# First tile of a CIN tower: part of slot a's third layer set ahead of slot b's first layer

## The chip, the cores and the metric

The kernel runs on one core of one Trainium2 chip. The metric is the device time of one execution, in microseconds. Of the kernel before there are three runs, 619.76, 620.20 and 620.31 us; the median is 620.2 us.

## The reference, cut to what matters

1024 samples each gather 32 embedding rows of 16 numbers. Three layers of a compressed interaction network follow, each a product with the samples' own embeddings and a contraction, and then a small three-layer network.

```python
x0 = embeddings                       # b samples, m = 32 fields, d = 16
xk = x0
for W in (W0, W1, W2):                # W: 32 x (32 or 64) x 64
    xk = relu(einsum('bmd,bhd,mhk->bkd', x0, xk, W))
    outs.append(sum(xk, axis=2))
z = concatenate(outs, axis=1)
h = relu(concatenate([z, dense_ctx], axis=1) @ W_top1 + b_top1)
h = relu(h @ W_top2 + b_top2)
y = h @ W_top3
```

All numbers are 32-bit floats.

## The kernel before, in words

**Streams and tiles.** The samples are cut into 16 streams of 64. Two streams make a tile: the even one uses slot a of every buffer, the odd one slot b. A stream's data is 1024 columns wide (64 samples by 16). Gathers (POOL, L323) fetch its embeddings, SP stores them in a DRAM scratch (L260), loads them back once as `base` (L278), and 16 more times shifted by different numbers of fields as the 16 chunks of `rolled` (L287).

**One layer.** A layer is a sum over chunks of (chunk of `rolled`) times (layer's input), multiplied by weights. DVE (VectorE) computes products of two chunks in one instruction (L406, into one of three `zd` buffers), reading the layer's input from PSUM (`xk_ps`). POOL (GpSimd) computes products of one chunk (L335, into one of four `zg` buffers), reading it from SBUF (`xk_sb`). PE (TensorE) accumulates them (L570), four matmuls for each chunk. The first layer has four chunks and the squares (L434, L579), the second and third have sixteen. ACT (ScalarE) then evacuates the sum (`evacuate`, L455 to L481): four copies into `xk_ps` and four into `xk_sb` (L472) as input of the next layer, and one into `relu_ab` (L481), which DVE later reduces (L382). For most layers `xk_sb` comes first, for the first layers of slot a `xk_ps`. A third layer is not evacuated this way, but summed by ACT (L451).

**The order.** It is written out by hand. `ORDER` lists phases (stream, layer, part); `CHUNKS` and `CHUNKS_AT` give for each part of a layer how many chunks DVE and how many POOL computes. Every engine runs the phases in the order of the list. In the first tile the phases are (0,0,0), (0,1,0), (1,0,0), (0,2,0), (1,1,0), (0,2,1). In the later tiles the order is another, and it repeats. In this document D0, D1, ... are DVE's product instructions in their order and G0, G1, ... POOL's: D4 to D10 and G0, G1 are (0,1,0); D11, D12 are (1,0,0); D13 to D15 and G2 are (0,2,0); D16 to D22 and G3, G4 are (1,1,0); D23 to D26 and G5 are (0,2,1); D27 begins (1,2,0).

**Gathers.** POOL issues all 256 gathers (16 for each stream) from its own queue, between its products. `GATHERS_AFTER_AT` and `GATHERS_AFTER` say how many follow each product: 4 after G0, 7 after G1, 3 after G2, 3 and 4 after G3 and G4, 7 after G5.

**Waits around the change.** DVE waits for `xk_ps` of the layer before (L397), or for the copy of `base` into `xk_ps` where the layer is the first (L394, made by ACT in `base_to_ps`), for the chunks of `rolled`, and for a free `zd` buffer (L401), that is for PE to have used the product three before. POOL waits for `xk_sb` (L355). A second and a third layer of a slot share one PSUM bank of `acc`, so PE begins the third only after the second was copied to `relu_ab`; this is a wait ahead of part 0 of layer 2. ACT's own order in the first tile is: squares of stream 0, evacuate (0,0), copy of base of stream 1, its squares, evacuate (0,1), (1,0), (1,1).

Of the kernel before, what the change touches and what calls it, by code (L numbers as in the profile page):

```python
# [24 lines left out]
STREAMS = BATCH // SAMPLES  # L25
# [20 lines left out]
CHUNKS = {(0, 0): [(4, 0)], (0, 1): [(4, 0), (10, 2)], (0, 2): [(12, 4)],  # L46
          (1, 0): [(4, 0)], (1, 1): [(14, 2)], (1, 2): [(4, 1), (8, 3)]}

CHUNKS_AT = {(0, 1): [(14, 2)], (0, 2): [(6, 1), (8, 1)], (STREAMS - 1, 2): [(12, 4)]}

ORDER = [(0, 0, 0), (0, 1, 0), (1, 0, 0), (0, 2, 0), (1, 1, 0), (0, 2, 1)]
for _t in range(1, TILES):
    ORDER += [(2 * _t - 1, 2, 0), (2 * _t, 0, 0), (2 * _t - 1, 2, 1), (2 * _t, 1, 0), (2 * _t + 1, 0, 0),
              (2 * _t, 1, 1), (2 * _t + 1, 1, 0), (2 * _t, 2, 0)]
ORDER += [(STREAMS - 1, 2, 0)]

# [3 lines left out]
GATHERS_FIRST = 24  # L60
GATHERS_EARLY = 8
GATHERS_AFTER = {(0, 1, 1): [3, 3], (1, 1, 0): [3, 3], (0, 2, 0): [3, 3, 2, 2], (1, 2, 0): [3], (1, 2, 1): [2, 2, 3]}
GATHERS_AFTER_AT = {(0, 1, 0): [4, 7], (0, 2, 0): [3], (1, 1, 0): [3, 4], (0, 2, 1): [7],
                    (STREAMS - 1, 2, 0): [0, 0, 0, 0]}

GATHERS_MORE = {(2 * t, 1, 1): 3 for t in range(1, 6)}
# [2 lines left out]
def chunks(stream, layer):  # L69
    return CHUNKS_AT.get((stream, layer), CHUNKS[stream % 2, layer])  # L70


class Plan:


    def __init__(self):
        self.dve, self.pool, self.merged = [], [], []
        nd = ng = 0
        for stream, layer, part in ORDER:
            parts = chunks(stream, layer)  # L80
# [23 lines left out]
def last_part(q):  # L104
    stream, layer, part = ORDER[q]
    return part == len(chunks(stream, layer)) - 1


def end_of(stream, layer):

    return ORDER.index((stream, layer, len(chunks(stream, layer)) - 1))


def by_act(stream, layer):

    return layer == 2 and stream < STREAMS - 1


def sums_to(stream, layer):

    return sum(last_part(q) and not by_act(*ORDER[q][:2]) for q in range(end_of(stream, layer) + 1))

# [24 lines left out]
def build_cin_tower(nc, ids, dense_t, tables, w0a, w0b, w12, wtop1, btop1, wtop2, btop2, wtop3, eye, out):  # L147
    with ExitStack() as ctx:
# [94 lines left out]
        def bank_of(stream, layer):  # L243
            return 2 if layer == 0 else stream % 2
# [69 lines left out]
        def _(pool):  # L314
# [12 lines left out]
            def product(q, n, j):  # L327
                stream, layer, _ = ORDER[q]
                s = stream % 2
                if n >= ZG_BUFS:  # L330

                    pool.wait_ge(zg_used, n - ZG_BUFS + 1)
                if layer == 1:
                    pool.wait_ge(rolled_in[s][j], 16 * (stream // 2 + 1))
                nc.gpsimd.tensor_tensor(zg[:, n % ZG_BUFS, :], rolled[:, s, j, :], xk_sb[:, s, :],  # L335
                                        ALU.mult).then_inc(zg_ready, 1)
# [5 lines left out]
            def gathers(n):  # L342
                nonlocal done
                for g in range(done, min(total, done + n)):
                    gather(g)
                    done = g + 1
# [5 lines left out]
            for q, (stream, layer, part) in enumerate(ORDER):  # L352
                if PLAN.pool[q]:

                    pool.wait_ge(xk_sb_ready, 4 * evacuations(*phase_before(stream, layer)))  # L355
                for x, (_, n, j, _) in enumerate(PLAN.pool[q]):
                    product(q, n, j)
                    gathers(GATHERS_AFTER_AT.get(ORDER[q], GATHERS_AFTER.get((stream % 2, layer, part)))[x])
                gathers(GATHERS_MORE.get(ORDER[q], 0))
# [62 lines left out]
        def _(act):  # L422
            def base_to_ps(i):
                s = i % 2
                if i > 1:

                    act.wait_ge(zd_ready, PLAN.dve[end_of(i - 2, 2)][-1][1] + 1)
                act.wait_ge(base_in, 16 * (i + 1))
                for h in range(2):
                    nc.scalar.copy(xk_ps[:, s, h * HALF:(h + 1) * HALF],  # L430
                                   base[:, h * HALF:(h + 1) * HALF]).then_inc(base_ps, 1)

            def squares(i):
                nc.scalar.activation(xk_sb[:, i % 2, :], base[:, :], ACT.Square).then_inc(squares_ready, 1)  # L434

            def wait_end(stream, layer):

                who, n, _, _ = PLAN.merged[end_of(stream, layer)][-1]
                act.wait_ge(zd_used if who == "dve" else zg_used, n + 1)
# [15 lines left out]
            def evacuate(stream, layer):  # L455
                s, bank = stream % 2, bank_of(stream, layer)
                wait_end(stream, layer)
                if layer < 2:
                    copies = [(xk_ps, xk_ps_ready), (xk_sb, xk_sb_ready)]
                    if (s, layer) != (0, 0):  # L460

                        copies.reverse()
                    for dst, ready in copies:
                        for h in range(2):
                            if (stream, layer, h) == (0, 0, 1):
                                if dst is xk_ps:

                                    continue

                                act.wait_ge(xk_ps_ready, 4)  # L470
                            for copy in range(2):
                                nc.scalar.activation(  # L472
                                    dst[copy * MAPS:(copy + 1) * MAPS, s, h * HALF:(h + 1) * HALF],
                                    acc[h * MAPS:(h + 1) * MAPS, bank, :], ACT.Relu).then_inc(ready, 1)
                if layer > 0:

                    act.wait_ge(reduced, sums_to(stream, layer - 1))
                elif stream > 1:

                    act.wait_ge(summed, stream - 1)  # L480
                nc.scalar.activation(relu_ab[:, s, :], acc[:, bank, :], ACT.Relu).then_inc(relu_ready, 1)  # L481
# [22 lines left out]
            act.wait_ge(base_in, 16)  # L504
            squares(0)
            evacuate(0, 0)
            base_to_ps(1)
            squares(1)
            evacuate(0, 1)
            evacuate(1, 0)  # L510
            evacuate(1, 1)
            act.wait_ge(const_in, const_count)
            for t in range(1, TILES):
                a, b, m = 2 * t, 2 * t + 1, t - 1
# [22 lines left out]
            m = TILES - 1  # L537
# [14 lines left out]
        def _(pe):  # L552
# [37 lines left out]
            def zsum(m):  # L590

                pe.wait_ge(reduced, sums_to(2 * m + 1, 1))
                pe.wait_ge(summed, 2 * (m + 1))
                if m > 0:
                    pe.wait_ge(y_ready, m)
                half_sums(m, mlp[0:MAPS, 0:TB], 0)
                half_sums(m, mlp[MAPS:P, 0:TB], 1)
                half_sums(m, mlp[0:MAPS, TB:2 * TB], 2).then_inc(zsum_done, 1)

            def mlp1(m):  # L600
                pe.wait_ge(zsum_sb, 2 * (m + 1))
                for c in range(H1 // P):
                    dst = mlp[:, c * TB:(c + 1) * TB]
                    nc.tensor.matmul(dst, wt1a[:, c * P:(c + 1) * P], z01[:, :], start=True, stop=False)  # L604
                    end = nc.tensor.matmul(dst, wt1b[:, c * P:(c + 1) * P], z2d[:, m * TB:(m + 1) * TB],  # L605
                                           start=False, stop=True)
                end.then_inc(h1_done, 1)

            def mlp2(m):
                pe.wait_ge(h1_sb, 4 * (m + 1))  # L610
                for c in range(H2 // P):
                    for k in range(H1 // P):
                        end = nc.tensor.matmul(mlp[:, c * TB:(c + 1) * TB], wt2[:, k, c * P:(c + 1) * P],  # L613
                                               h1[:, k, :], start=(k == 0), stop=(k == H1 // P - 1))
                end.then_inc(h2_done, 1)

            def mlp3(m):
                pe.wait_ge(h2_sb, 2 * (m + 1))
                for k in range(H2 // P):
                    end = nc.tensor.matmul(mlp[0:1, 0:TB], wt3[:, k:k + 1], h2[:, k, :],  # L620
                                           start=(k == 0), stop=(k == H2 // P - 1))
                end.then_inc(y_done, 1)
# [6 lines left out]
                half_sums(TILES - 1, stage[0:MAPS, 0:TB], 0)  # L629
                half_sums(TILES - 1, stage[MAPS:P, 0:TB], 1).then_inc(last_z01_done, 1)  # L630

            for q in range(6):
                phase(q)
            for m in range(TILES - 1):
                q = 6 + 8 * m
                for x in range(5):
                    phase(q + x)
                phase(q + 5, {2: lambda: zsum(m), 5: lambda: mlp1(m)})
                phase(q + 6, {2: lambda: mlp2(m), 6: lambda: mlp3(m)})
                phase(q + 7)  # L640
            phase(len(ORDER) - 1, {6: last_sums})

            m = TILES - 1
# [70 lines left out]
```

## Time and profile before

| | |
|---|---|
| median of three runs | 620.2 us |
| the profiled execution, device time | 619.78 us |
| its span, first to last instruction | 618.0 us |
| mean granted TensorE clock | 0.994 of full speed |
| PE busy | 562.0 us |
| DVE busy | 554.5 us |
| POOL busy | 468.6 us |
| ACT busy | 299.5 us |

Times in the profile are counted from the start of the span. POOL is the engine that both computes and issues gathers; the 0.30 us between two gathers are not counted as busy. D4 starts at 42.23 us; the first tile's products end on DVE at about 101.4 us, where D27 follows.

### The profile page before, as it was taken

To read this page: it belongs to the slowest core of one execution; us is meant where nothing else is said; L and a number is where in the kernel's file an instruction comes from. 1 tells how busy PE (TensorE), PEld (TensorE's weight loads), DVE (VectorE), ACT (ScalarE), POOL (GpSimd) and SP (SyncE) were. 2 spreads that over 40 slices of the span, in tenths; PEclk is the share of its full clock that TensorE was granted. 3 is DMA by queue.
4 is the path that set the end of the run, shared out by engine and by line. 5 is a ranking of instruction groups with operands and counts; after the bars stand their busy time and mean duration, and the time that the engine had idled before them with its cause. 6 is when DMAs were issued, how large, how long until landed. Compare 5 with 4: busy or idle time off the path is not lost.

```text
span 618.0 us, 8180 instructions
## 1 busy us (share of the span) xinstructions
PE 562.0 (91%) x2752; PEld 206.1 (33%) x2752; DVE 554.5 (90%) x281; ACT 299.5 (48%) x1366; POOL 468.6 (76%) x354
## 2 busy tenths in 40 slices
PE   0058889999999999999999999899998999999997
PEld 0012222334333443334333433234332433334334
DVE  0067899999999999999999999989998999999991
ACT  0021607574357535674366535674346544774331
POOL 6748888888888888888888888888888885125450
PEclk9998999999999999999999999999999999999999
DMA  6297979792699819893699719793498809892000
GB/s 171 79 382 254 394 250 396 241 397 82 209 359 330 294 51 374 297 399 108 218 351 339 299 40 379 265 400 130 171 397 309 329 3 319 316 406 100 1 2 0
DMA packets 54252, 152.02 MB, mean 246 GB/s; under 512 B 9697, under 2 KB 18913, under 8 KB 54210
## 3 DMA queue, kind: packets, MB, share of 16 engines
q1 hardware_dynamic: 46018, 149.39, 64.7%
q0 software_dynamic: 8192, 2.11, 2.6%
q8 instruction: 21, 0.34, 0.2%
q14 instruction: 21, 0.17, 0.1%
HBM read 147.26 MB, written 4.20 MB: 245 GB/s over the span
## 4 chain that ended last, share of the span: by engine, by line
PE 48%; POOL 23%; DVE 10%; issue 9%; DMA 6%; SPq 1%; ACT 1%; DVEq 0%; POOLq 0%
PE acc L570 43%; POOL emb L323 14%; DVE zd L406 10%; POOL zg L335 9%; DMA rolled<-x_scratch 5%; PE mlp L613 2%; SPq L287 1%; PE mlp L604 1%; PE mlp L605 1%; PE acc L579 1%; PE mlp L620 0%; DVE zpart L382 0%; PE mlp L586 0%; ACT xk_sb L472 0%; DMA emb<-tables_in,index 0%
## 5 line engine op out<-in xcount | busy, mean ns | idle before, releaser
L406 DVE TENSOR_TENSOR zd<-rolled,xk_ps 128x2048 f32<-128x2048 f32 x239 | 530.0, 2279 | 16.2 <-PE acc L570 9.2
L570 PE MATMUL acc<-zd,w_sb 128*64 128x512 f32 x1672 | 384.6, 597 | 8.4 <-DVE zd L406 8.4
L323 POOL DMA_INDIRECT emb<-tables_in,index x256 | 244.6, 955 | 75.3 <-issue 64.3
L335 POOL TENSOR_TENSOR zg<-rolled,xk_sb 128x1024 f32<-128x1024 f32 x94 | 223.8, 2382 | 52.0 <-ACT xk_sb L472 18.9
L570 PEld LDWEIGHTS acc<-zd,w_sb 128*64 128x64 f32 x1672 | 119.7, 138 | 242.5 <-issue 210.4
L472 ACT ACTIVATE xk_sb<-acc 64x512 f32<-64x512 f32 x128 | 75.7, 591 | 64.4 <-PE acc L570 61.9
L570 PE MATMUL acc<-zg,w_sb 128*64 128x512 f32 x376 | 98.6, 601 | 6.9 <-POOL zg L335 6.9
L570 PE MATMUL acc<-zd,w 128*64 128x512 f32 x256 | 61.6, 601 | 37.4 <-DVE zd L406 37.4
L472 ACT ACTIVATE xk_ps<-acc 64x512 f32<-64x512 f32 x126 | 71.8, 570 | 30.1 <-PE acc L570 27.2
L451 ACT ACTIVATE relu_ab<-acc 128x16 f32<-128x16 f32 x480 | 78.9, 294 | 8.3 <-PE acc L570 8.3
L451 ACT ACTIVATION_READ_ACCUMULATOR relu_ab<-acc 128x1 f32 x480 | 79.3, 322 | 0.0
L434 ACT ACTIVATE xk_sb<-base 128x1024 f32<-128x1024 f32 x16 | 16.9, 1056 | 67.6 <-PE acc L570 39.2
L570 PEld LDWEIGHTS acc<-zg,w_sb 128*64 128x64 f32 x376 | 26.9, 137 | 58.3 <-issue 41.8
L570 PEld LDWEIGHTS acc<-zd,w 128*64 128x64 f32 x256 | 18.7, 139 | 74.3 <-issue 71.6
L430 ACT COPY xk_ps<-base 128x512 f32<-128x512 f32 x30 | 16.6, 587 | 45.4 <-DVE zd L406 28.2
L406 DVE TENSOR_TENSOR zd<-rolled,base 128x1024 f32<-128x1024 f32 x4 | 4.9, 1225 | 27.9 <-DMA rolled<-x_scratch 27.7
L382 DVE TENSOR_REDUCE zpart<-relu_ab 128x32 f32<-128x512 f32 x33 | 22.3, 677 | 5.2 <-ACT relu_ab L481 5.2
L491 ACT ACTIVATE h<-mlp,bt 128x128 f32<-128x128 f32 x28 | 8.0, 368 | 38.8 <-PE mlp L605 38.8
L481 ACT ACTIVATE relu_ab<-acc 128x512 f32<-128x512 f32 x33 | 19.7, 597 | 9.4 <-PE acc L570 8.6
L502 ACT COPY z2d_y<-mlp 1x128 f32<-1x128 f32 x7 | 1.8, 254 | 36.4 <-PE mlp L620 36.4
L579 PE MATMUL acc<-xk_sb,w 128*64 128x512 f32 x64 | 17.2, 613 | 0.0
L613 PEld LDWEIGHTS mlp<-h,wt 128*128 128x128 f32 x112 | 13.0, 191 | 5.7 <-issue 5.7
(45 smaller groups left out, 101.0 us busy)
## 6 DMA issues: line engine op xcount, KB each, us to landing
rolled<-x_scratch SPq DMA_DIRECT2D x256, 512.0 KB, 9.4
base<-x_scratch SPq DMA_DIRECT2D x16, 512.0 KB
emb<-tables_in,index POOLq DMA_INDIRECT x256
x_scratch<-emb SPq DMA_DIRECT2D x32, 128.0 KB
w_sb<-w_in SPq DMA_DIRECT2D x2, 512.0 KB, 4.9
wt<-wtop_in SPq DMA_DIRECT2D x1, 512.0 KB, 6.3
wt1a<-wtop_in SPq DMA_DIRECT2D x1, 256.0 KB, 5.5
w<-w0a_in SPq DMA_DIRECT2D x1, 160.0 KB, 2.3
```

The source lines that it names most:

```text
L323: pool.indirect_dma_start(emb[:, i % 2, c * DIM:(c + 1) * DIM], None, tables, bass.IndirectOffsetOnAxis(index[:, g:g + 1].bitcast(U32), 0) ...
L335: nc.gpsimd.tensor_tensor(zg[:, n % ZG_BUFS, :], rolled[:, s, j, :], xk_sb[:, s, :], ALU.mult).then_inc(zg_ready, 1)
L382: nc.vector.tensor_reduce(zpart[:, t % 2, layer, s, :], relu_ab[:, s, :].rearrange("p (b d) -> p b d", d=DIM), AX_X, ALU.add).then_inc(red ...
L406: nc.vector.tensor_tensor(zd[:, n % ZD_BUFS, 0:w, :], rolled[:, s, j:j + w, :], repeated(layer_in, w), ALU.mult).then_inc(zd_ready, 1)
L430: nc.scalar.copy(xk_ps[:, s, h * HALF:(h + 1) * HALF], base[:, h * HALF:(h + 1) * HALF]).then_inc(base_ps, 1)
L434: nc.scalar.activation(xk_sb[:, i % 2, :], base[:, :], ACT.Square).then_inc(squares_ready, 1)
L451: end = nc.scalar.activation(relu_ab[:, s, cols], acc[:, s, cols], ACT.Relu, accum_out=zpart[:, t % 2, 2, s, b:b + 1])
L472: nc.scalar.activation(dst[copy * MAPS:(copy + 1) * MAPS, s, h * HALF:(h + 1) * HALF], acc[h * MAPS:(h + 1) * MAPS, bank, :], ACT.Relu).th ...
L481: nc.scalar.activation(relu_ab[:, s, :], acc[:, bank, :], ACT.Relu).then_inc(relu_ready, 1)
L570: end = nc.tensor.matmul(acc[h * MAPS:(h + 1) * MAPS, bank, :], weights, z[:, h * HALF:(h + 1) * HALF], start=(j + c == 0), stop=(i == len ...
L579: nc.tensor.matmul(acc[h * MAPS:(h + 1) * MAPS, bank, :], w0[:, L0CH, :], xk_sb[:, s, h * HALF:(h + 1) * HALF], start=False, stop=False)
L613: end = nc.tensor.matmul(mlp[:, c * TB:(c + 1) * TB], wt2[:, k, c * P:(c + 1) * P], h1[:, k, :], start=(k == 0), stop=(k == H1 // P - 1))
```

## The change

Slot a's third layer in the first tile is cut in three parts in place of two: (4,0), (6,1), (4,1) in place of (6,1), (8,1), the first number DVE's chunks and the second POOL's. The first part, four chunks, is set ahead of (1,0,0); the second stands behind it, ahead of (1,1,0); the third is behind (1,1,0). ACT evacuates (0,1) ahead of the copy of stream 1's base, and of (0,1) it fills `xk_ps` first. G0 has 1 gather behind it in place of 4 and G2 has 6 in place of 3. The order of the later tiles is the same, and their products keep their numbers from D27 and G6 on.

```diff
-CHUNKS_AT = {(0, 1): [(14, 2)], (0, 2): [(6, 1), (8, 1)], (STREAMS - 1, 2): [(12, 4)]}
-
-ORDER = [(0, 0, 0), (0, 1, 0), (1, 0, 0), (0, 2, 0), (1, 1, 0), (0, 2, 1)]
+CHUNKS_AT = {(0, 1): [(14, 2)], (0, 2): [(4, 0), (6, 1), (4, 1)], (STREAMS - 1, 2): [(12, 4)]}
+
+ORDER = [(0, 0, 0), (0, 1, 0), (0, 2, 0), (1, 0, 0), (0, 2, 1), (1, 1, 0), (0, 2, 2)]
+HEAD = len(ORDER)
...
-GATHERS_AFTER_AT = {(0, 1, 0): [4, 7], (0, 2, 0): [3], (1, 1, 0): [3, 4], (0, 2, 1): [7],
+GATHERS_AFTER_AT = {(0, 1, 0): [1, 7], (0, 2, 1): [6], (1, 1, 0): [3, 4], (0, 2, 2): [7],
...
-                    if (s, layer) != (0, 0):
+                    if (s, layer) != (0, 0) and (stream, layer) != (0, 1):
                         copies.reverse()
...
             squares(0)
             evacuate(0, 0)
+            evacuate(0, 1)
             base_to_ps(1)
             squares(1)
-            evacuate(0, 1)
             evacuate(1, 0)
             evacuate(1, 1)
...
-            for q in range(6):
+            for q in range(HEAD):
                 phase(q)
             for m in range(TILES - 1):
-                q = 6 + 8 * m
+                q = HEAD + 8 * m
```

With the new order D11 and D12 are (0,2,0); D13, D14 are (1,0,0); D15 to D17 and G2 are (0,2,1); D18 to D24 and G3, G4 are (1,1,0); D25, D26 and G5 are (0,2,2).

## Rows read from the trace of the kernel before

**Rows 1.** The page, busy time of each engine.

```profile
PE 562.0 (91%) x2752; PEld 206.1 (33%) x2752; DVE 554.5 (90%) x281; ACT 299.5 (48%) x1366; POOL 468.6 (76%) x354
```

**Rows 2.** The page, the chain that ended last, by engine and by line.

```profile
PE 48%; POOL 23%; DVE 10%; issue 9%; DMA 6%; SPq 1%; ACT 1%; DVEq 0%; POOLq 0%
PE acc L570 43%; POOL emb L323 14%; DVE zd L406 10%; POOL zg L335 9%; DMA rolled<-x_scratch 5%; PE mlp L613 2%; SPq L287 1%; PE mlp L604 1%; PE mlp L605 1%; PE acc L579 1%; PE mlp L620 0%; DVE zpart L382 0%; PE mlp L586 0%; ACT xk_sb L472 0%; DMA emb<-tables_in,index 0%
```

**Rows 3.** POOL's waits, 74 to 505 us: total us, times, longest.

```profile
POOL emb L323 <- issue: 52.0, 204, 0.3
...
POOL zg L335 <- ACT xk_sb L472: 0.6, 1, 0.6
```

**Rows 4.** PE's waits, the first row 74 to 310 us, the second 310 to 473.

```profile
PE acc L570 <- DVE zd L406: 4.2, 13, 0.9
...
PE acc L570 <- POOL zg L335: 4.2, 5, 1.7
```

**Rows 5.** Timeline of all engines: start, duration, what; in brackets idle before.

```profile
469.88 2.37 POOL L335 TENSOR_TENSOR zg<-rolled,xk_sb 128x1024 f32<-128x1024 f32 x1
...
472.30 1.08 PE L570 MATMUL acc<-zg,w_sb 128*64 128x512 f32 x4 [1.65 <-POOL zg L335]
```

**Rows 6.** Timeline of POOL: G0, G1, G2, G3.

```profile
48.80 2.39 POOL L335 TENSOR_TENSOR zg<-rolled,xk_sb 128x1024 f32<-128x1024 f32 x1
...
56.09 2.38 POOL L335 TENSOR_TENSOR zg<-rolled,xk_sb 128x1024 f32<-128x1024 f32 x1
...
67.12 2.37 POOL L335 TENSOR_TENSOR zg<-rolled,xk_sb 128x1024 f32<-128x1024 f32 x1
...
73.69 2.38 POOL L335 TENSOR_TENSOR zg<-rolled,xk_sb 128x1024 f32<-128x1024 f32 x1 [0.56 <-ACT xk_sb L472]
```

**Rows 7.** Timeline of DVE: D9 and D10, D11, D12, D13 on, D18 to D27.

```profile
53.82 4.47 DVE L406 TENSOR_TENSOR zd<-rolled,xk_ps 128x2048 f32<-128x2048 f32 x2
64.08 2.29 DVE L406 TENSOR_TENSOR zd<-rolled,xk_ps 128x2048 f32<-128x2048 f32 x1 [5.78 <-DMA rolled<-x_scratch]
66.85 2.29 DVE L406 TENSOR_TENSOR zd<-rolled,xk_ps 128x2048 f32<-128x2048 f32 x1 [0.48 <-DMA rolled<-x_scratch]
69.45 6.68 DVE L406 TENSOR_TENSOR zd<-rolled,xk_ps 128x2048 f32<-128x2048 f32 x3 [0.32 <-ACT xk_ps L472]
...
81.64 22.05 DVE L406 TENSOR_TENSOR zd<-rolled,xk_ps 128x2048 f32<-128x2048 f32 x10
```

**Rows 8.** Timeline of PE, 44 to 69 us.

```profile
44.57 7.04 PE L570 MATMUL acc<-zd,w_sb 128*64 128x512 f32 x24 [3.85 <-DVE zd L406]
...
52.30 3.60 PE L570 MATMUL acc<-zd,w_sb 128*64 128x512 f32 x16
58.52 1.98 PE L570 MATMUL acc<-zg,w_sb 128*64 128x512 f32 x4 [2.62 <-POOL zg L335]
...
66.51 1.94 PE L570 MATMUL acc<-zd,w 128*64 128x512 f32 x8 [1.96 <-DVE zd L406]
```

**Rows 9.** Timeline of ACT, 59 to 74 us.

```profile
59.31 1.11 ACT L430 COPY xk_ps<-base 128x512 f32<-128x512 f32 x2 [14.42 <-DMA base<-x_scratch]
...
64.61 2.44 ACT L472 ACTIVATE xk_sb<-acc 64x512 f32<-64x512 f32 x4 [3.20 <-PE acc L570]
67.07 2.35 ACT L472 ACTIVATE xk_ps<-acc 64x512 f32<-64x512 f32 x4
69.45 0.60 ACT L481 ACTIVATE relu_ab<-acc 128x512 f32<-128x512 f32 x1
71.17 2.44 ACT L472 ACTIVATE xk_sb<-acc 64x512 f32<-64x512 f32 x4 [1.13 <-PE acc L570]
```

**Rows 10.** Busy time by stretch: PE, PEld, DVE, ACT, POOL, then clock, DMA, GB/s.

```profile
48.00:52.00 4.00, 4.00 (x22) 1.39 (x20) 4.00 (x3) 0.00 (x0) 3.74 (x3) 1.00 0.98 370
58.50:61.50 3.00, 2.98 (x8) 1.01 (x10) 0.00 (x0) 2.10 (x3) 2.26 (x3) 0.50 0.97 262
44.60:47.90 3.30, 3.30 (x8) 0.97 (x10) 3.30 (x2) 0.29 (x1) 2.39 (x4) 0.50 1.04 392
```

## The prediction

> **What bounds the kernel now.** I read the page's busy times first. PE stands at 91%, DVE at 90%, POOL at 76% [rows 1], so PE and DVE look like the pair to watch. The page's chain says something else: POOL has 23% of it, gathers 14 and products 9 [rows 2], while the gathers ahead of the first layer can account for about 5 of these (24 us of 618).
>
> So I read POOL's waits. From 74 to 505 us it waited for others only 0.6 us; the rest is 204 gaps of 0.3 us at most between its own gathers [rows 3], which the page doesn't count as busy. POOL runs solidly from G3 at 73.69 us [rows 6] to the last gathers. Whether that matters is read from PE's waits: up to 310 us it waits for DVE alone (4.2 us in 13 waits), from 310 to 473 us for POOL alone (4.2 us in 5 waits) [rows 4]. The last is at 472.3: G69 ends at 469.88 + 2.37 = 472.25, and PE, idle for 1.65 us, takes it at 472.30 [rows 5]. Behind it PE and DVE set the pace to the end. So POOL has a lead in the early tiles and loses it until the products of POOL arrive last. The end of the kernel is G69 plus a constant, and G69 is **G3 plus a constant**, as long as POOL has no idle time between. When G3 starts is thus the question; DVE's gaps in the first tile matter only if POOL's lead is not used up.
>
> What set G3 before: 0.56 us of waiting for `xk_sb` of (1,0) [rows 6], whose copies began at 71.17 [rows 9], when PE had finished (1,0,0).
>
> **The change part by part.** I follow the chain from G0 at 48.80, which nothing changed comes before.
>
> *Gathers and G1.* G0 ends at 51.19. Four gathers fill the 4.90 us up to G1, seven the 8.65 from 58.47 to 67.12 [rows 6]: 1.25 for each more. One gather takes 1.15, so G1 runs 52.34 to 54.72, not to 58.47. Before, PE stood 2.62 us for G1 [rows 8]; this wait goes. PE takes a chunk in 0.86 us (16 matmuls in 3.60, less a tail of 0.17, are 4 chunks [rows 8]). D7 and D8 keep it until 55.74, G1 to 56.60, D9 to 58.32. What is late next is D10 from DVE: it ends at 53.82 + 4.47 = 58.29 [rows 7]. A product of two chunks that PE takes at once is out 1.94 us after [rows 8]: (0,1) is complete at 60.3, and was at 64.6 [rows 9]. Gain here 4.3 us.
>
> *Evacuation of (0,1).* `xk_ps` first: 60.32 + 2.35 = 62.67, then `xk_sb` to 65.11, then `relu_ab` (0.60) to 65.74 [rows 9]. The copy of base, 1.11, was made at 59.31 [rows 9] and is now behind it, 65.76 to 66.87, with the squares to 67.9. It is wanted by D13, below, at 67.10: hidden by 0.2 us, and what it is late by beyond that DVE waits.
>
> *POOL up to G2.* 54.72 + 8.65 = 63.37, but `xk_sb` is there at 65.11: G2 at 65.19, having waited 1.8 us, a new idle. G2 ends at 67.57; six gathers (7.40) lead to 74.97. The number of gathers ahead of G3 is as before, 14.
>
> *(0,2,0) on DVE.* D11 can start at 62.70 in place of 64.08, when the first chunks of stream 1 landed [rows 7]. Starts are 2.20 apart (ten in 22.05 [rows 7]): D12 at 64.90, D13 at 67.10, ended 69.38, D14 at 69.30, ended 71.57. Stream 1's chunks landed at 64.08 and 66.85 at the latest, and SP's queue issues them as before, since neither stream 1's gathers nor its loads are touched: no wait for D13 and D14. But they are (1,0,0), which G3 needs, and end 2.4 us later than D12 did (66.85 + 2.29 = 69.14).
>
> *The added wait.* PE may begin (0,2,0) only when `relu_ab` of (0,1) is read, at 65.74. Everything on PE queues behind it: D11 to 67.52, D12 to 69.24, then D13 (0.15 behind DVE: 69.53), the squares (0.86), D14 at 72.12, out at 74.04. DVE sees it through the three buffers: D14 needs D11 used, 67.6, in time.
>
> *G3.* ACT starts at 74.08 on `xk_sb` of (1,0) and ends at 76.52, G3 starts at 76.60. That is **2.91 us later** than 73.69; POOL was free at 74.97.
>
> *TensorE's clock.* This sum has PE at its higher clock. Yet PE now idles from 60.28 to 65.80, 5.5 us. The trace: after an idle of 3.85 us and after one of 2.62 the granted clock is 0.50 (1.2 GHz), beside 1.00 (2.4 GHz) at 48 to 52 us [rows 8, 10]; after 1.96 us it did not fall [rows 8]. So D11 will run slowly. Price: D4 to D6, six chunks, took 7.04 us where six at 0.86 and the tail are 5.33: 1.7 lost. G1, D9, D10, five chunks, began at 58.52 and were out at 64.57 (ACT at 64.61 [rows 9]): 6.05 for 4.47, 1.6 lost. Bounds: nothing, and 3.4 if D12 runs slowly too. I take 1.5, near the two rows and a little under them, since both stretches were full of work and the new one may end sooner. D12 is then done at 70.74 and not 69.24, D13 starts at 70.74 and not 69.53. This adds 1.2: G3 at 77.8.
>
> The Trainium skill (TensorE: Matmul & The Clock Gate, Part 1: The HAM clock gate) says that the stretch at the lower clock after a restart is not tied to the kernel's start and differs from run to run. No row here can show that, from one execution; by it the 1.2 may be anything from nothing up in a single run, and the total between the sum without it and mine.
>
> *DVE after that.* The evacuation of (1,0) now ends (`xk_ps`) 77.7 + 2.44 + 2.35, so D18 waits till about 80.2. D24 is the last of (1,1). Behind it stand only D25 and D26, 4.4 us, where four products, 8.8 us, stood; from D24's end to `xk_ps` of (1,1) are 1.94 + 2.44 + 2.35 and hand-overs of 0.12, 6.85 us. So DVE idles about 2.4 us ahead of D27. Before, D27 started at 81.64 + 9 x 2.20 = 101.4 [rows 7]. Now D24 starts at 80.2 + 6 x 2.20 + 0.60 (the reduction) = 94.0, ends at 96.3, and D27 starts at 103.1: 1.7 later; with the clock up, 0.4 later. All idle that DVE saves (5.78 + 0.48 + 0.32 = 6.6 us [rows 7]) it pays again. This lies beside POOL's delay, which is longer.
>
> *POOL after G3.* Same products, same gathers. From G3 to G6 are three products (7.2 us) and 3, 4 and 7 gathers (3.65, 4.90, 8.65), so POOL is at G6 at 102.2, and `xk_sb` of (1,1) is ready at about 100.8 (D24's end, 1.94, 2.44 and hand-overs): no regain, and no further wait. Stream 2's gathers end with G3's second, 4 us later; its loads into `base` are issued 4 us later, at 89, and first used at about 105.
>
> **The sum.** 2.9 + 1.2 = 4.1 us on POOL's chain. Span 618.0 + 4.1 = 622.1, device time 619.8 + 4.1 = 623.9. The median of the runs is 0.4 above the profiled execution: 620.2 + 4.1 = **624.3 us**, 0.7% slower.
>
> **Rivals.**
>
> *A. POOL's lead absorbs it.* PE and DVE carry the end, and only D27's shift counts: +0.4 to +1.7, 620.6 to 621.9. For: POOL is busy 76% and PE waited for it 4.2 us only. Against: rows 3 and 4 together, no idle and a wait at 472 us. It decides if G69 has room.
>
> *B. Faster: DVE carries the end and its gap stays closed.* The price is DVE's idle, 6.6 us before and 62.70 - 58.29 = 4.4 after, so -2.2: 618.0. It decides from the point where D27 starts before 101.4, at 99.2, which needs `xk_ps` of (1,1) 4.4 us after D24 and not 6.85, and where POOL has over 3 us to spare at G69. Speaks for it: DVE's 90%; against it, the rows for both conditions. The Trainium skill (Perfetto Trace Analysis, Identifying the Most-Contended Engine) says to find by occupancy the engine that limits, and to close that engine's gaps; by this it would be DVE rather than POOL, whose gaps between gathers the occupancy leaves out, and B would hold.
>
> *C. The waits come out as before.* The low clock or the landing of stream 1 moves so that G3 is near 73.7: within 1.2 us of before. Little speaks for it, as D14 ends after D12 did by DVE's pace alone.
>
> *D. More: low clock through D12 as well*, 3.4 for 1.5: +6.0, 626.2. It is the upper part of the forecast's mechanism.
>
> **How the numbers follow.** Forecast with D 0.83, A 0.06, B 0.06, C 0.05. Within 0.2% (1.24 us, about what a measurement of this kernel tells from no change) lies C and over half of A. So faster 0.06, same 0.09, slower 0.85. The range goes from the bottom of the forecast (623.1 with the clock at full) down into A, 621.9, and up to D, 626.2.
>
> **What would show it.** G1 near 52.3 with no wait of PE for it; G2 near 65.2; PE idle near 60.3 to 65.8 and a granted clock of 0.5 behind; G3 near 77.8 (76.6 if the clock stays up); D27 near 103; POOL without waits from there to 500 us; PE waiting for POOL well ahead of 310 us, and at G69 at about 476.4. Wrong would be a wait of POOL behind G3, a last PE wait for POOL ahead of G69, or G3 before 76.

## The result

The changed kernel takes **624.3 us** (median of six runs, 623.57 to 626.33), the kernel before 619.75 us beside it (six runs, 619.16 to 620.31). The ratio is 1.0077 with a 95% interval of 1.0061 to 1.0093: slower by 0.8%. The profiled execution took 623.57 us with a span of 621.7 us, 3.7 more than before.

First the page of the changed kernel: engines, and the chain that ended last, as in [rows 1, 2].

```profile
PE 563.4 (91%) x2752; PEld 207.9 (33%) x2752; DVE 554.7 (89%) x281; ACT 299.7 (48%) x1366; POOL 468.5 (75%) x354
...
PE 53%; POOL 21%; DVE 8%; issue 8%; DMA 7%; ACT 3%; SPq 1%; DVEq 0%; POOLq 0%
```

Busy times are nearly the same (PE has 1.4 us more), and the chain's shares have moved by five points at most; neither says where the 3.7 us come from. The difference is in who waited. POOL's timeline after (G0, G1, G2, G3, G69), which answers to [rows 5, 6]:

```profile
48.37 2.39 POOL L336 TENSOR_TENSOR zg<-rolled,xk_sb 128x1024 f32<-128x1024 f32 x1
...
51.92 2.38 POOL L336 TENSOR_TENSOR zg<-rolled,xk_sb 128x1024 f32<-128x1024 f32 x1
65.06 2.36 POOL L336 TENSOR_TENSOR zg<-rolled,xk_sb 128x1024 f32<-128x1024 f32 x1 [2.12 <-ACT xk_sb L473]
77.69 2.36 POOL L336 TENSOR_TENSOR zg<-rolled,xk_sb 128x1024 f32<-128x1024 f32 x1 [2.89 <-ACT xk_sb L473]
473.72 2.37 POOL L336 TENSOR_TENSOR zg<-rolled,xk_sb 128x1024 f32<-128x1024 f32 x1
```

G1 is 4.2 us earlier than before, G3 4.0 later, G69 3.84 later. The two idles in brackets are new: 5.0 us, where 0.56 stood. Then come the waits of POOL from 78 to 509 us, and those of PE in three stretches, 74 to 260, 260 to 310, 310 to 477; they answer to [rows 3, 4]. POOL's 2.9 us are those ahead of G3 itself. Behind G3 its gaps between gathers are 0.3 us at most, and its one wait for another engine, the 0.4 us of the last row, stands at 507.79 us, behind G69.

```profile
POOL emb L324 <- issue: 51.5, 202, 0.3
POOL zg L336 <- ACT xk_sb L473: 2.9, 1, 2.9
...
POOL zg L336 <- PE acc L571: 0.4, 1, 0.4
```

```profile
PE acc L571 <- DVE zd L407: 5.9, 8, 2.6
...
PE acc L571 <- POOL zg L336: 0.5, 1, 0.5
...
PE acc L571 <- POOL zg L336: 4.4, 4, 1.7
PE acc L571 <- DVE zd L407: 0.5, 2, 0.3
```

PE after: D11 and D12, D27, G6, and G69 (which PE takes 0.05 us after POOL has made it, as in [rows 5]):

```profile
65.65 5.18 PE L571 MATMUL acc<-zd,w_sb 128*64 128x512 f32 x16 [5.53 <-ACT relu_ab L482]
...
105.40 2.83 PE L571 MATMUL acc<-zd,w_sb 128*64 128x512 f32 x8 [2.55 <-DVE zd L407]
107.95 1.94 PE L571 MATMUL acc<-zg,w_sb 128*64 128x512 f32 x4
...
476.14 0.65 PE L571 MATMUL acc<-zg,w_sb 128*64 128x512 f32 x2 [1.67 <-POOL zg L336]
```

The granted clock of three stretches after (the figure 0.50 or 1.00 near the end of the row, that is 1.2 or 2.4 GHz), columns as in [rows 10]:

```profile
65.70:68.70 3.00, 3.00 (x8) 0.95 (x10) 3.00 (x2) 2.02 (x3) 2.70 (x2) 0.50 1.03 404
70.00:77.00 7.00, 7.00 (x34) 2.25 (x32) 7.00 (x5) 1.77 (x3) 3.77 (x4) 1.00 1.03 394
...
106.40:109.70 3.30, 3.30 (x11) 1.08 (x9) 3.30 (x3) 3.30 (x45) 2.98 (x3) 0.50 1.03 396
```

The sixteen matmuls from 65.65 took 5.18 us where the same number took 3.60 at the full clock [rows 8]: 1.58 lost. The clock was low a second time, from 106.4 us on, behind the 2.55 us of idle ahead of D27.

DVE's three waits in the first tile after, which took the place of those in [rows 7]:

```profile
62.55 11.10 DVE L407 TENSOR_TENSOR zd<-rolled,xk_ps 128x2048 f32<-128x2048 f32 x5 [4.42 <-ACT xk_ps L473]
...
80.02 4.49 DVE L407 TENSOR_TENSOR zd<-rolled,xk_ps 128x2048 f32<-128x2048 f32 x2 [1.38 <-ACT xk_ps L473]
...
102.97 6.68 DVE L407 TENSOR_TENSOR zd<-rolled,xk_ps 128x2048 f32<-128x2048 f32 x3 [2.49 <-ACT xk_ps L473]
```

### The profile page after: what moved, and what is told of

It is laid out like the page before. It is cut to its first block, busy times and chain, and to the rows that moved or that the text cites. A ratio compares the mean times of both kernels' runs of the same rounds, so it can differ in the third digit from the quotient of the medians.

```text
span 621.7 us, 8181 instructions
## 1 busy us (share of the span) xinstructions
PE 563.4 (91%) x2752; PEld 207.9 (33%) x2752; DVE 554.7 (89%) x281; ACT 299.7 (48%) x1366; POOL 468.5 (75%) x354
## 3 DMA queue, kind: packets, MB, share of 16 engines
q0 software_dynamic: 8192, 2.11, 2.9%
## 4 chain that ended last, share of the span: by engine, by line
PE 53%; POOL 21%; DVE 8%; issue 8%; DMA 7%; ACT 3%; SPq 1%; DVEq 0%; POOLq 0%
PE acc L571 47%; POOL emb L324 12%; POOL zg L336 9%; DVE zd L407 8%; DMA rolled<-x_scratch 6%; PE mlp L614 2%; ACT xk_sb L473 1%; ACT xk_ps L473 1%; SPq L288 1%; PE acc L580 1%; PE mlp L605 1%; PE mlp L606 1%; PE mlp L621 0%; PE mlp L587 0%; DMA emb<-tables_in,index 0%
## 5 line engine op out<-in xcount | busy, mean ns | idle before, releaser
L336 POOL TENSOR_TENSOR zg<-rolled,xk_sb 128x1024 f32<-128x1024 f32 x94 | 223.7, 2382 | 56.3 <-ACT xk_sb L473 24.4
L571 PEld LDWEIGHTS acc<-zd,w_sb 128*64 128x64 f32 x1672 | 121.0, 138 | 249.5 <-issue 212.6
```

The source lines that it names most:

```text
L571: end = nc.tensor.matmul(acc[h * MAPS:(h + 1) * MAPS, bank, :], weights, z[:, h * HALF:(h + 1) * HALF], start=(j + c == 0), stop=(i == len ...
```

## The experiments

Ratios are to the kernel before, timed on the same chip in the same rounds, with 95% intervals; each has five rounds. L336 is the product of POOL where L335 was before.

### Is the end G3 plus a constant?

**Two gathers more ahead of G69**, in the kernel before:

```diff
-(1, 1, 0): [3, 4]
+(1, 1, 0): [5, 4]
```

> The kernel before, with two more gathers behind G3 (5 in place of 3), the order of everything else untouched. They are taken from the end of the list, where POOL idles, so the number of gathers is the same, but two more lie ahead of G69. Theory, POOL's chain carries the end: 2 x 1.25 us later at G69 and at the end, +2.5 us (the clock and DVE's order play no part). Rival, PE and DVE carry the end and POOL's lead absorbs such delays: within 0.3 us of before.

Measured: 1.0105 (1.0082 to 1.0127), 625.9 us and 6.2 more than before; single times from 623.4 to 628.5. The profiled execution, the fastest (623.36), has a span 3.5 us longer, and shows what I had left out:

```profile
466.49 0.98 POOL L323 DMA_INDIRECT emb<-tables_in,index  x1 [1.50 <-DMA x_scratch<-emb]
...
473.51 2.38 POOL L335 TENSOR_TENSOR zg<-rolled,xk_sb 128x1024 f32<-128x1024 f32 x1
```

G3 was at 73.49, so G69 came 400.0 us behind it; before it was 396.2. The excess of 3.8 is 2.5 for the gathers and 1.2 for a wait: gathers two further ahead reached a buffer whose store had not landed. DVE meanwhile was hardly later than before: its row that ends with D27 starts at 82.00, where [rows 7] have 81.64.

```profile
82.00 22.06 DVE L406 TENSOR_TENSOR zd<-rolled,xk_ps 128x2048 f32<-128x2048 f32 x10
```

The direction is the theory's, and 2.5 us of the price; a POOL lead that absorbs such a delay is refuted. The size was missed, with 3.5 in the profiled execution and 6.2 by the medians. Where the slower executions lost the other 3 us isn't shown, since none of them was profiled; a longer wait of the same kind is a guess.

**The gathers' split undone** in the changed kernel:

```diff
-(0, 1, 0): [1, 7], (0, 2, 1): [6]
+(0, 1, 0): [4, 7], (0, 2, 1): [3]
```

> The changed kernel with the gathers split as before: 4 behind G0 and 3 behind G2. Theory: G1 is back at 56.1, PE stands for it until 58.5 and takes it, D9 and D10 at the lower clock, (0,1) is complete at 64.6, D11 starts at about 67.0 in place of 62.6, and G3 comes 4.4 us later than in the changed kernel, at about 82; the end follows by 4.4 (3.8 to 5): about 628.7. Rival (the gathers' split is of no account for the end, since the number ahead of G3 is the same): no change from 624.3.

Measured: 1.0121 (1.0101 to 1.0141), 628.2 us; by the ratios 2.7 us more than the changed kernel, less than the 3.8 to 5 expected, and in the profiled executions 4.7 (span 626.4). POOL's G3 and G69, then D11 and D12 on PE:

```profile
81.95 2.35 POOL L336 TENSOR_TENSOR zg<-rolled,xk_sb 128x1024 f32<-128x1024 f32 x1 [8.08 <-ACT xk_sb L473]
...
478.17 2.37 POOL L336 TENSOR_TENSOR zg<-rolled,xk_sb 128x1024 f32<-128x1024 f32 x1
```

```profile
68.47 6.62 PE L571 MATMUL acc<-zd,w_sb 128*64 128x512 f32 x16 [5.54 <-ACT relu_ab L482]
```

The number of gathers ahead of G3 is the same in both. What moved G3 is PE's work, which G1 holds up. That G3 came where it was expected (81.95, expected about 82) is partly luck. The clock did not fall behind PE's wait for G1 in this execution (1.00 from 58.4 to 62.8 us), so DVE began D11 only 2.8 us later than in the changed kernel, at 65.36 where 67.0 was expected. The other 1.4 us are D11 and D12 on PE: 6.62 us here and 5.18 there. The 2.8 alone are close to what the ratios say.

**The gathers' split alone**, in the kernel before:

```diff
-(0, 1, 0): [4, 7], (0, 2, 0): [3]
+(0, 1, 0): [1, 7], (0, 2, 0): [6]
```

> The kernel before with the new split of gathers alone (1 behind G0, 6 behind G2). Theory: G1 at 52.3, PE's wait of 2.6 us and the fall of its clock go, (0,1) complete at 60.3, DVE waits for rolled alone; but G3 is reached by POOL at 73.7 as before and its chain is full, so the end stays: within 0.3 us of before (619.7). Rival (PE's and DVE's idle in the first tile is worth its time at the end): 1 to 2 us faster.

Measured: 1.0005 (0.9992 to 1.0017). The profile has G1 at 51.79 and no wait of PE for it, and the end is within 0.5 us of where it was:

```profile
74.30 2.36 POOL L335 TENSOR_TENSOR zg<-rolled,xk_sb 128x1024 f32<-128x1024 f32 x1 [1.34 <-ACT xk_sb L472]
...
470.51 2.37 POOL L335 TENSOR_TENSOR zg<-rolled,xk_sb 128x1024 f32<-128x1024 f32 x1
```

One thing was not foreseen: PE now idled from 60.3 to 64.7, ahead of (1,0,0), its clock fell there instead (D11's eight matmuls took 3.68 us, against the 1.94 of [rows 8]), and G3 came 0.6 later.

**`xk_sb` of (0,1) first**, in the changed kernel:

```diff
-if (s, layer) != (0, 0) and (stream, layer) != (0, 1):
+if (s, layer) != (0, 0):
     copies.reverse()
```

> The changed kernel with xk_sb of (0,1) copied first, as before, xk_ps after it. Theory: D11 starts 2.4 us later, at about 65.0, PE idles until 67.4 and takes D11 at the lower clock, D14 is taken at about 75.1 in place of 73.2, G3 comes at about 79.6, 1.9 us later, and the end with it: 626.2 (625.8 to 626.8). Rival (POOL gains by having xk_sb, and G2, 2.3 us earlier): the end earlier than 624.3 or equal.

Measured: 1.0104 (1.0080 to 1.0127), 626.5 us; by the ratios 1.7 more than the changed kernel, where 1.9 was expected. G2 came at 62.66 without a wait, and did not help:

```profile
79.29 2.36 POOL L336 TENSOR_TENSOR zg<-rolled,xk_sb 128x1024 f32<-128x1024 f32 x1 [6.88 <-ACT xk_sb L473]
...
475.40 2.38 POOL L336 TENSOR_TENSOR zg<-rolled,xk_sb 128x1024 f32<-128x1024 f32 x1
```

Put together, profiled executions only:

| kernel | G3 | G69 - G3 | span | span - G3 |
|---|---|---|---|---|
| before | 73.69 | 396.19 | 618.0 | 544.3 |
| split alone | 74.30 | 396.21 | 618.5 | 544.2 |
| changed, five matmuls (below) | 77.24 | 396.21 | 621.5 | 544.3 |
| changed | 77.69 | 396.03 | 621.7 | 544.0 |
| changed, ten matmuls (below) | 79.23 | 396.15 | 623.4 | 544.2 |
| changed, `xk_sb` first | 79.29 | 396.11 | 623.4 | 544.1 |
| changed, split undone | 81.95 | 396.22 | 626.4 | 544.4 |

Seven kernels of two orders, G3 over a range of 8.3 us, and the span follows it within 0.5. The five of the new order could not tell POOL's chain from DVE's by themselves: both G3 and D18 wait for copies of (1,0), and D27 starts 25.3 us behind G3 in all five. What tells them apart is a change in which the two move differently. From the kernel before to the changed one D27 is 1.6 us later (101.4 and 102.97) and G3 4.0, and the span grows by 3.7. With two gathers more D27 is 0.4 later and G69 3.6, and the span grows by 3.5. Both times the span goes with POOL.

### What the clock costs

Extra matmuls ahead of PE's wait for `relu_ab`, into a bank unused there:

```diff
 elif layer == 2 and part == 0:
+    if stream == 0:
+        for k in range(10):      # 5 in the second run
+            nc.tensor.matmul(mlp[0:MAPS, :], w12_sb[:, 0, k, :],
+                             w12_sb[:, 1, 0:8, :].rearrange("p j k -> p (j k)"), start=True, stop=True)
     pe.wait_ge(relu_ready, sums_to(stream, 1))
```

> The changed kernel with ten extra matmuls of 128x64 by 128x512, into a bank that nothing uses there, ahead of PE's wait for relu_ab of (0,1), so that PE is busy for 4.3 of the 5.5 us that it idled. Theory: the granted clock stays at 1.00, D11's pair takes 1.7 and not 3.3 us, D13 starts at once behind DVE, G3 starts 1.2 us earlier (about 76.5) and the end comes 1.2 us earlier (1.0 to 1.5). Rival (the clock's stretch is hidden beside DVE's own pace): no change of G3 and of the end.

Measured: 1.0085 (1.0070 to 1.0100), slower than the changed kernel if anything. The experiment failed by its size; PE in the profiled execution:

```profile
60.19 8.32 PE L566 MATMUL mlp<-w_sb 128*64 128x512 f32 x19
```

It kept the clock at 1.00, and kept PE from D11 until 67.9. With five:

> The changed kernel with five (not ten) extra matmuls ahead of PE's wait for relu_ab of (0,1). Ten took 7.7 us in place of the 4.3 that I had reckoned, since all wrote the same half of the bank and could not run in pairs, and D11 began 2.3 us later than in the changed kernel; five should end at about 64.3, ahead of the wait's end at 65.6. Theory (the lower clock costs 1.2 of the 4 us): granted clock 1.00 at 65 to 69 us, D11 and D12 at 1.7 us each, G3 at about 76.5 (77.69 in the changed kernel), the end 1.2 us earlier, about 623.1. Rival (the clock costs nothing): G3 and the end as in the changed kernel, 624.3.

Measured: 1.0037 (1.0022 to 1.0052), 622.7 us; beside the changed kernel's 1.0077, 2.5 us less. PE, and the clock behind it:

```profile
60.74 4.46 PE L566 MATMUL mlp<-w_sb 128*64 128x512 f32 x10
66.45 3.65 PE L576 MATMUL acc<-zd,w_sb 128*64 128x512 f32 x16 [1.26 <-ACT relu_ab L482]
```

```profile
66.40:70.20 3.80, 3.69 (x18) 1.12 (x19) 3.80 (x3) 2.10 (x3) 3.35 (x3) 1.00 1.05 407
```

The sixteen matmuls take 3.65 us and not 5.18. Counted from G0, G3 comes at 28.64 and not at 29.32: 0.7 us in these two executions, where 1.2 was expected. But 0.6 of the difference arose earlier: PE was done with (0,1) 0.6 us later after G0, before the first extra matmul. Counted from D11's start on PE (66.45 and 65.65), G3 comes 10.79 and not 12.04 us later, 1.25 less, which is the price that was expected. By the ratios it is 2.5, with intervals that reach from 0.6 to 4.4. The mechanism is shown. Its price differs from one execution to another: the same sixteen matmuls, at full clock 3.60, took 5.18 us here, 5.79 with `xk_sb` first and 6.62 with the split undone.

### POOL relieved

Five gathers fewer ahead of G69, in both kernels, and in two mended versions:

```diff
-GATHERS_MORE = {(2 * t, 1, 1): 3 for t in range(1, 6)}
+GATHERS_MORE = {(2 * t, 1, 1): 2 for t in range(1, 6)}
```

> The kernel before with 2 in place of 3 gathers at the end of each (even stream, second layer) of tiles 1 to 5: five gathers fewer ahead of G69, 6.25 us of POOL. Theory: POOL no longer gates PE; the end comes earlier by what PE lost beside a tile of 69.36 us, that is G69's place moves from 472.3 to about 468.3: -4.0 us. Rival (POOL is not what carries the end): no change, or slower if the later gathers make loads late.

> The changed kernel with the same five gathers fewer ahead of G69. Theory: with POOL relieved what is left of the change's loss is the shift of D27 (101.42 to 102.97), so it ends 1.5 us (1 to 2) behind the kernel before with the same edit, and about 6.5 us ahead of the changed kernel. Rival (the loss is TensorE's lower clock or DVE's waits by themselves, whatever POOL does): the distance stays at 4 to 4.5 us.

Measured: the old order 0.9967 (0.9954 to 0.9979), 617.6 us, 2.0 less than before; the new order 1.0026 (1.0007 to 1.0044), 621.0. PE's waits from 74 to 477 us, old order, then new:

```profile
PE acc L570 <- issue: 2.7, 9, 0.5
PE acc L570 <- DVE zd L406: 1.9, 5, 0.9
```

```profile
PE acc L571 <- DVE zd L407: 6.4, 9, 2.6
PE acc L571 <- issue: 1.0, 4, 0.3
```

POOL is gone from both, and both are faster, so it did carry the end. But the sizes are off: 2.0 gained for 4.0 expected, and a distance of 3.4 where I had expected 1.5. The rival expected 4 to 4.5, and 3.4 is nearer to it: with POOL relieved most of the loss stays, as delays of PE and DVE by themselves. In the two profiled executions D27 starts at 100.15 and 103.61, 3.5 us apart and not 1.5. The single times tell part of why the gain is small: 614.9 to 619.6 in the old order (twelve runs), while those of the kernel before beside it lie between 618.9 and 621.7 (23 runs). With POOL as the limit, PE and DVE can lose some us in the first tile unseen (before, PE waits 4.2 us for POOL later on [rows 4]); without it an execution would show what it lost there. The wider spread fits this, but no run here isolates it.

> A version meant to beat both: the kernel before (its order) with the new split of gathers (1 and 6), five extra matmuls ahead of (1,0,0) so that PE's clock stays up, and 2 in place of 3 gathers at the end of each even stream's second layer in tiles 1 to 5. Theory: POOL is relieved, so now PE's and DVE's saving in the first tile counts: the relief alone was worth 2.0 us, PE's fall of clock and DVE's wait for xk_ps 0.5 to 1.5 more: 2.5 to 3.5 us faster than before, ratio 0.995 to 0.996, and a narrower spread of single times than the relief alone had (614.9 to 619.6). Rival: what is left is bound by the loads of rolled, and the first tile's saving is lost in them: ratio 0.997 as with the relief alone.

> The same with 1 in place of 3 gathers: ten gathers fewer ahead of G69. Theory: POOL's tile is then 68.8 us and shorter than the 69.36 of PE and DVE, POOL never gates PE; equal to or up to 1 us faster than the version with 2. Rival: gathers come so late that the stores and loads of later streams are late, and it is slower than the version with 2, at worst slower than before.

> The changed order with POOL relieved (2 in place of 3) and PE kept at its clock (five extra matmuls). Theory: what remains of the change is DVE's wait of 2.5 us ahead of D27 and little else, and it ends 1 to 2 us behind the version of the old order with the same three edits; against before about -1 to -2 us. Rival (the new order has another cost that neither POOL nor the clock explains): 3 us or more behind it.

The first two are the old order, the new split, five matmuls ahead of (1,0,0), and 2 or 1 in place of 3; the third the new order with five matmuls and 2. Measured: 0.9935 (0.9920 to 0.9950), 615.9 us; 0.9946 (0.9930 to 0.9963), 616.2 us; 0.9974 (0.9962 to 0.9985), 618.6 us. **The first beats both kernels, by 4.0 us and by nearly 9**, where 2.5 to 3.5 were expected over the kernel before. One gather fewer still neither helps nor harms. The new order stays 2.4 us behind the old with the same helps by the ratios, 2.7 by the medians, between the 1 to 2 expected and the rival's 3. DVE of the new order (third), then of the old (first), D9 to D27:

```profile
54.23 4.47 DVE L407 TENSOR_TENSOR zd<-rolled,xk_ps 128x2048 f32<-128x2048 f32 x2
63.13 11.08 DVE L407 TENSOR_TENSOR zd<-rolled,xk_ps 128x2048 f32<-128x2048 f32 x5 [4.42 <-ACT xk_ps L473]
...
102.31 2.29 DVE L407 TENSOR_TENSOR zd<-rolled,xk_ps 128x2048 f32<-128x2048 f32 x1 [2.49 <-ACT xk_ps L473]
```

```profile
64.26 2.29 DVE L406 TENSOR_TENSOR zd<-rolled,xk_ps 128x2048 f32<-128x2048 f32 x1 [3.65 <-DMA rolled<-x_scratch]
67.14 8.88 DVE L406 TENSOR_TENSOR zd<-rolled,xk_ps 128x2048 f32<-128x2048 f32 x4 [0.59 <-DMA rolled<-x_scratch]
...
81.52 22.06 DVE L406 TENSOR_TENSOR zd<-rolled,xk_ps 128x2048 f32<-128x2048 f32 x10
```

4.42 + 2.49 = 6.9 us idle against 3.65 + 0.59 = 4.2. These 2.7 are as much as the distance of the medians and of the two spans (618.8 and 616.1), but that they are its cause isn't shown. The old order's execution began D4 1.9 us later (44.54, the other 42.64), so its D27 is only 1.0 us ahead (101.3 and 102.31), and 1.7 of the 2.7 arise behind D27. There DVE of the new order waits longer for `rolled`, 2.6 us from 300 to 500 us against 1.2; where that comes from is open.

## Why the prediction was right

The mechanism was right: G3's start is the question, the wait for `relu_ab` and the low clock behind it move it, and POOL hands the delay on to the end. Step by step, with what the changed kernel showed:

- *G1.* 3.55 us behind G0 (foreseen 3.54); PE's wait for it gone.
- *G2.* 65.06 (65.19), idle ahead 2.12 (1.8).
- *The added wait.* PE idle 5.53 us (5.5), until 65.65.
- *The clock.* Fell, 1.58 us lost on D11 and D12 (1.5 taken). D13 was taken 0.1 us ahead of what was foreseen, and G3 came at 77.69 (77.8). But G0 was 0.43 us earlier here than in the trace of before; counted from G0, G3 came after 29.3 us, where 29.0 were foreseen.
- *POOL's chain.* No wait between G3 and G69; PE's first wait for POOL at 262 us, its last for G69, made at 476.09 and taken at 476.14 (476.4).
- *The sum.* Span 621.7 (622.1), device time 623.57 (623.9), median 624.3 (624.3). The ratio's interval puts the loss between 3.8 and 5.8 us; 4.1 is in it.

That the median is met to the digit is luck. The forecast added 4.1 to 620.2; the kernel before has 619.75 in six runs, so the loss is 4.55 by the medians and 4.8 by the ratio, a little more than was foreseen. The clock's term is luck in part as well: 1.5 was taken and 1.58 came, but other profiled executions with this order lost 1.8 (POOL relieved), 2.2 (`xk_sb` first) and 3.0 us (split undone) on the same sixteen matmuls.

Three slips in the working changed nothing. 24 us of 618 are 4%, not about 5. The line on DVE adds 77.7 + 2.44 + 2.35, though 77.7 is already the end of the copies into `xk_sb`; its 80.2 is 77.7 and 2.35 and hand-overs, and D18 came at 80.02. And POOL waited once more before 505 us, 0.4 us for PE, behind G69.

The choice that decided was to follow POOL and not the two engines with 90%. Rival A falls with PE's waits after 260 us and with the two gathers. Rival B, faster by 2.2 us, did not come. Something like its price shows only in the old order with POOL relieved, where the new split and the five matmuls took the median from 617.6 to 615.9 us; how much of that is DVE's idle and how much the clock isn't told apart. Rival C fell with G3. Rival D fell in this execution, where the clock was back at 1.00 from 69.0 us, as D12 began; but its size can occur, since with the split undone 3.0 of its 3.4 us were lost. What the Trainium skill says of occupancy (Perfetto Trace Analysis, Identifying the Most-Contended Engine) doesn't hold here: the engine with 76% carried the end. The 52 us of gaps between its gathers [rows 3] don't count in the 76%, though it waited for no other engine in them; and the share is taken over the whole span, while POOL's solid stretch ends near 509 us.

Two points were missed. The second fall of the clock, at 106 us, was not in the forecast; from D27 to D28 PE took 4.3 us where 2.6 is usual, under POOL's delay, which is longer. And D27's shift, 1.7 us in rival A and 1.5 in the experiment's expectation, was taken as the whole of what the change costs where POOL has room; with POOL relieved it was 2.4 to 3.4.

## What to carry to other kernels

Look for the engine that never waits, not for the one that is busiest: issue gaps are no idle, and a chain without a wait hands any delay at its head to the end. Before an order is changed to close one engine's gap, write down the start of the first instruction behind which that chain has no wait, and ask first what the change does to it. And where an engine with little slack hides another's gaps, relieve it first; here the split alone gained nothing (1.0005), and it was part of the best version once POOL was relieved.

## What the runs showed of the hardware

After an idle of PE its clock does not fall in every execution. In the old order with POOL relieved PE idled 3.85 us ahead of D4 and 2.11 ahead of G1, and the stretches behind ran at 1.00, where [rows 10] have 0.50 (the first idle is as long as the one in [rows 8], the second half a microsecond shorter):

```profile
44.60:47.90 3.30, 1.94 (x8) 0.48 (x8) 3.30 (x3) 1.39 (x3) 2.38 (x4) 1.00 1.02 385
58.50:61.50 3.00, 2.94 (x14) 1.06 (x16) 0.95 (x1) 1.73 (x3) 2.23 (x4) 1.00 0.93 306
```

This was the fastest of its twelve runs (614.88 us, median 617.6). Of the thirteen profiled executions of this case all idled for 3.85 or 3.86 us ahead of D4, and the clock fell behind it in ten; the other two in which it did not are those of the split undone and of the old order with five matmuls and 2. The last had a mean clock of 1.000 and was still the slowest of its six (617.9 us), so the clock alone doesn't make an execution fast. Nor does the length of the idle decide alone: behind 2.35 us the clock fell (two gathers more, ahead of G1), behind 2.65 it did not (this execution, ahead of D11). By what the Trainium skill states (TensorE: Matmul & The Clock Gate, Part 1: The HAM clock gate) the low stretch differs from run to run; the traces agree, and here it can be missing altogether.

Matmuls that write the two halves of a bank in turn took 3.60 us for sixteen [rows 8], 0.22 us each. The ten extra calls, twenty matmuls in the trace and all into one half, started 0.43 us apart, from 60.19 to 68.34, with the granted clock at 1.00. That it is the one half that makes the difference is likely, but no run varied it alone.
